# Mixer network on one Trainium2 core: the last batch's row lists summed on TensorE from one-hots, and the second expert stage's first loads reordered

## The reference, cut to what matters

```python
logits = x @ gate_weight.T                 # 2048 tokens, 128 experts
logits = where(old_to_new == -1, -inf, logits)
top_v, top_i = top_k(softmax(logits), 8);  top_v /= sum(top_v)
flat_e = old_to_new[top_i].reshape(-1)     # 48 kept experts
oh  = flat_e[:, None] == arange(48)
pos = sum(cumsum(oh, axis=0) * oh, axis=-1) - 1     # place within the expert
valid = pos < 192
xb[flat_e, pos] = x[tok]
g, u = split(einsum('ech,eoh->eco', xb, gate_up_proj))
y = einsum('eci,ehi->ech', silu(g) * u, down_proj)
final[tok] += y[flat_e, pos] * top_v * valid
x = layernorm(x + final)
```

## Time and profile before

| | |
|---|---|
| median of 3 runs | 2162.5 us (2161.75 to 2166.09) |
| time of the profiled execution | 2158.87 us |
| its span | 2157.1 us |
| PE busy | 1739.3 us (81%) |
| DVE busy | 1523.6 us (71%) |
| ACT busy | 956.8 us (44%) |
| POOL busy | 1086.7 us (50%) |

### The profile page before, as it was taken

The page is one execution under the profiler, slowest core; times in us unless marked ns, Lnnn a source line. Parts: engine busy times, 40 slices in busy tenths (PEclk is TensorE's granted clock), DMA queues, the critical chain, the costliest instruction groups (busy, mean ns, idle before and its releaser), DMA issues. The chain is left out here.

```text
span 2157.1 us, 34592 instructions
## 1 busy us (share of the span) xinstructions
PE 1739.3 (81%) x9155; PEld 1383.7 (64%) x9156; DVE 1523.6 (71%) x2883; ACT 956.8 (44%) x1867; POOL 1086.7 (50%) x817
## 2 busy tenths in 40 slices
PE   4898989347999999999998888788832079999990
PEld 3566565236888888888886555555421078888880
DVE  4477777765777888887884323788879757777774
ACT  4355452312444444444443324444423157777773
POOL 1000624564667667667676000044538657777763
PEclk9899989657999999999999898888865589999995
DMA  8011111035888888888896613131010369999967
GB/s 322 28 40 59 31 48 40 1 122 152 206 208 212 205 227 211 223 228 212 218 231 153 198 21 59 59 59 59 1 59 23 126 194 256 258 250 256 257 149 254
DMA packets 138553, 318.80 MB, mean 148 GB/s; under 512 B 30713, under 2 KB 31321, under 8 KB 136825
## 3 DMA queue, kind: packets, MB, share of 16 engines
q1 hardware_dynamic: 71448, 201.74, 27.1%
q0 software_dynamic: 64752, 112.04, 26.8%
q10 hardware_dynamic: 2288, 4.29, 0.5%
HBM read 238.68 MB, written 97.62 MB: 156 GB/s over the span
## 5 line engine op out<-in xcount | busy, mean ns | idle before, releaser
L98 POOL DMA_INDIRECT tab_rows<-pair,slot x256 | 313.7, 1226 | 452.6 <-DVEq L752 296.6
L90 PE MATMUL gu<-wgu_h,xgT_h 128*128 x648 | 233.5, 360 | 7.3 <-DVE xgT_l L1428 3.7
L1253 POOL DMA_INDIRECT xg<-x_rows,ids x167 | 191.5, 1147 | 62.5 <-issue 48.5
L90 PE MATMUL gu<-wgu_l,xgT_h 128*128 x648 | 219.6, 339 | 0.0
L90 PE MATMUL gu<-wgu_h,xgT_l 128*128 x648 | 218.3, 337 | 0.0
L1308 ACT ACTIVATE ysb<-yp,wts 128x512 f32<-128x512 f32 x160 | 110.1, 688 | 144.7 <-PE yp L1535 144.7
L90 PE MATMUL guk<-xgT_hk,wgu_hk 128*128 128x192 f32 x576 | 161.7, 281 | 0.0
L90 PE MATMUL guk<-xgT_lk,wgu_hk 128*128 128x192 f32 x576 | 158.8, 276 | 0.0
L90 PE MATMUL guk<-xgT_hk,wgu_lk 128*128 128x192 f32 x576 | 158.8, 276 | 0.0
L1298 ACT ACTIVATE sg<-gu 128x192 f32<-128x192 f32 x162 | 53.6, 331 | 235.1 <-PE gu L90 235.1
L1428 DVE TENSOR_TENSOR xgT_l<-tpx,xgT_h 128x512 fp32r<-128x512 f32 x163 | 112.2, 688 | 55.6 <-ACT xgT_h L1294 53.4
(11 more groups left out here) (503 smaller groups left out, 5043.3 us busy)
## 6 DMA issues: line engine op xcount, KB each, us to landing
wgu_sb<-in_wgu SPq DMA_DIRECT2D x64, 768.0 KB
wgu_sbk<-in_wgu SPq DMA_DIRECT2D x48, 768.0 KB, 4.4
wd_sb<-in_wd SPq DMA_DIRECT2D x64, 256.0 KB
wd_sbk<-in_wd SPq DMA_DIRECT2D x48, 256.0 KB, 5.3
ct<-in_ctxT SPq DMA_DIRECT2D x8, 1024.0 KB, 5.0
wd_sb<-in_wd SPq DMA_DIRECT2D x64, 128.0 KB
wd_sbk<-in_wd SPq DMA_DIRECT2D x48, 128.0 KB, 5.8
odd_rows<-zero SPq DMA_DIRECT2D x1, 4352.0 KB, 15.5
```

Source lines behind the costliest of these rows:

```text
L90: i = nc.tensor.matmul(out, left(k), right(k), start=(start and k == 0 and m == 0), stop=(k == ops - 1 and m == 2))
L98: nc.gpsimd.indirect_dma_start(out=tab, out_offset=bass.IndirectOffsetOnAxis(ap=s["slot"][:, n:n + 1].bitcast(U32), axis=0), in_=s["pair"] ...
L1253: nc.gpsimd.indirect_dma_start(out=xg[:, t % G, :], out_offset=None, in_=x, in_offset=bass.IndirectOffsetOnAxis(ap=ids[:, t:t + 1].bitcast ...
```

## The change

1. The last batch's four tiles are routed together, as the other batches are. Its pairs are not scattered. SP loads the table as it is after three batches (in a tile of `x3`), ahead of the last batch's stores; DVE makes its token numbers float before it routes.
2. `hot` of the last batch lies in `parts`, a bf16 tile of 32 choices x 5 values x 48 experts, experts innermost: the one-hot itself, the one-hot times the token number, and the one-hot times the weight in three bf16 pieces. For each choice, `spots` is the one-hot of its position among 192 places. 64 products on TensorE (32 choices, places in two groups of 128 and 64) sum `spots` transposed times `parts` over tokens and choices in one PSUM tile, which holds for each place and expert the row number and weight. `lists_taken` adds them to the transposed table of the three batches and writes `ids` and `wts`, which now are made before `kept_experts` starts.
3. `kept_experts` starts with the gathers. The rows are cleared in four parts, one per expert pair of halves, and gathers wait for their part alone. ACT and DVE take expert 0's rows before its weights. SP requests the third expert's weights when the rows of the first two experts have landed.

```diff
@@ kept_experts, SP @@
                 if e >= 2:
                     sp.wait_ge(s_wt[e % 2], e // 2 * 48)
+                if e == 2:
+                    for m in range(2):
+                        sp.wait_ge(s_g[m], 32)
@@ kept_experts, POOL @@
-            scatter(nc, tab, s, E1 * REG1 - 1, s_lot, BT - 1)
...
+                elif t % 2 == 0:
+                    pool.wait_ge(s_clear, t // 2 + 1)
...
-            pool.wait_ge(s_tab, 3)
@@ kept_experts, ACT @@
             for n in range(2):
+                copy_xT(0, n)
                 gate_up_upper(0, n, False)
                 down_upper(0, n, False)
-            act.wait_ge(s_lot, SCAT)
-            nc.scalar.dma_start(lot[:, :, :].rearrange("t n o -> t (n o)"),
-                                tab.rearrange("(r n) o -> r (n o)", n=P)[0:T1, :]).then_inc(s_rows, 16)
-            copy_xT(0, 0)
-            copy_xT(0, 1)
@@ kept_experts, DVE @@
-            nc.vector.memset(xg[:, :, :], 0.0).then_inc(s_tab, 1)
+            for n in range(NF):
+                nc.vector.memset(xg[:, 2 * n:2 * n + 2, :], 0.0).then_inc(s_clear, 1)
...
             for n in range(2):
+                split_xT(0, n)
                 gate_up_lower(0, n)
                 down_lower(0, n)
@@ mixer_two, SP @@
+                        sp.wait_ge(s_scat, (B - 1) * (16 * BT * TOPK))
...
+                        sp.dma_start(lot.rearrange("t n o -> t (n o)"),
+                                     d["tab1"].rearrange("(r n) o -> r (n o)", n=P)[0:T1, :]).then_inc(s_lot, 16)
@@ mixer_two, POOL @@
+            nc.gpsimd.iota(places[:, :], [[1, CAP]], base=0, channel_multiplier=0,
...
-            for j in range(BT - 1):
-                pool.wait_ge(s_idx, B + j + 1)
-                settle(pool, passed)
-                scatter(nc, d["tab1"], drain, E1 * REG1 - 1, s["lot"][1], j, j + 1)
@@ mixer_two, DVE, drained @@
-                for j in range(BT):
-                    route_j(j)
-                    slots_j(j)
...
+                dve.wait_ge(s_lot, 16)
+                c.done(nc.vector.tensor_copy(lotf, lot[:, :, 0]))
+                routed()
+                parts_made()
+                spots_made()
+                lists_taken()
@@ mixer_two, DVE, parts_made @@
+                    c.done(nc.vector.tensor_tensor(parts[:, :, 1, :].rearrange("p (j k) e -> p e j k", k=TOPK),
+                                                   own.rearrange("p e (j k) -> p e j k", k=TOPK),
+                                                   tok16[:, :].unsqueeze(1).unsqueeze(3).to_broadcast([P, E1, BT, TOPK]), ALU.mult))
...
+                    c.done(nc.vector.tensor_tensor(parts[:, :, 2:5, :].rearrange("p n v e -> p v e n"), own.unsqueeze(1).to_broadcast([P, 3, E1, NP]),
+                                                   w16[:, :, :].unsqueeze(2).to_broadcast([P, 3, E1, NP]), ALU.mult))
@@ mixer_two, DVE, spots_made @@
+                    for n in range(NP):
+                        nc.vector.tensor_scalar(spots[:, n, :], places[:, :], pos8[:, n:n + 1], None, ALU.is_equal).then_inc(s_spot, 1)
@@ mixer_two, PE, drained @@
+                for n in range(NP):
+                    pe.wait_ge(s_spot, n + 1)
+                    for m, (lo, w) in enumerate(((0, P), (P, IR))):
+                        i = nc.tensor.matmul(tb[0:w, m, 0:5 * E1].rearrange("p (v e) -> p v e", e=E1), spots[:, n, lo:lo + w],
+                                             parts[:, n, :, :], start=(n == 0), stop=(n == NP - 1))
+                i.then_inc(s_list, 1)
```

More of the change, by code:

```diff
@@ L1576, in kept_experts @@
         ysb = sb("ysbk", [P, G, D])
-        lot = sb("lotk", [T1, P, 2], I32)
-        lotf = sb("lotfk", [T1, P])
-        ids = sb("idsk", [P, T1], I32)
-        wts = sb("wtsk", [P, T1])
+        ids, wts = s["ids"], s["wts"]
         tpx = ps("tpxk", [P, 2, 512])
@@ L2361, in norm3, with route_rows @@
                 assert c.n == N2, c.n
-            def route_rows(c, js, logits, at):
+            def route_rows(c, js, logits, hot):
                 rows = slice(js[0] * TOPK, (js[-1] + 1) * TOPK)
@@ L2448, in route @@
                 dve.wait_ge(s_lg, b + (ROUTED + 1))
-                yield from route_rows(c, range(BT), lgp, 0)
+                yield from route_rows(c, range(BT), lgp, hot)
                 assert c.n == KRT, c.n
@@ L2473, in drained @@
                 stat, mv, rstd, shift = stats[2]
+                own = parts[:, :, 0, :].rearrange("p n e -> p e n")
                 c.done(nc.vector.tensor_scalar(tokf[:, :], tokf[:, :], float(S), None, ALU.add))
+                c.done(nc.vector.tensor_scalar(back[:, :], s["tcol"][:, 0:1], -1.0, -float(2 * P), ALU.mult, ALU.add))
                 dve.wait_ge(s_x4, B * BT)
@@ L2518, in drained @@
                 scaled(3)
-                for j in range(BT):
-                    route_j(j)
-                    slots_j(j)
-                with nc.allow_low_precision("small counts"):
-                    for j in range(BT):
-                        c.done(nc.vector.tensor_tensor(s["macc1"][:, :], s["macc1"][:, :], mask[:, j, :], ALU.add))
-                        c.wait()
+                dve.wait_ge(s_lot, 16)
[4 more added lines that the diff above has]
+                lists_taken()
             norm1(0, True)
@@ L2870, in program @@
         mixer_one(nc, d, s)
+        sb, _, _ = alloc(nc, ctx)
+        s.update(ids=sb("idsk", [P, T1], I32), wts=sb("wtsk", [P, T1]))
         with ExitStack() as held:
```

146 lines of the change are left out of this document (91 added, 55 removed).

## The result

| | kernel before | changed kernel |
|---|---|---|
| median (lowest to highest), us | 2162.12 (2155.89 to 2166.09), 4 runs | 2201.85 (2196.46 to 2206.18), 4 runs |
| ratio, 95% interval | 1 | 1.0185 [1.0151, 1.0219] |
| profiled execution: its time, its span | 2158.87, 2157.1 | 2203.19, 2201.3 |
| mark (lower half of expert 3's weights on DVE) | 1751.46 | 1789.16 |
| mark to the end of the span | 405.6 | 412.1 |

The change makes the kernel 39.7 us slower. The forecast was no difference, and the time lies far outside its range. Of the 44.2 us between the two spans 37.7 have gathered by the mark.

What follows compares the result with a forecast made beforehand. Bound: the path through POOL's last 32 scatters and the table's load to the second expert stage's even pace. First gather 12.6 us earlier, 6.3 given back, 5.7 lost to strided reads: 0.6 faster, 2161.9 us; own range 2158.5 to 2165.5, overall 2154.5 to 2168.

Steps and rivals of the forecast that it cites:

- load of the table, start of the routing: After DVE's last scatter lands, SP loads the 96 KB table in 2.2 us with its issue; routing starts at 1677.65.
- routing up to `mask`'s end, with the strides: DVE routes four tiles in the third batch's 14.56 us, +0.8 for strided `hot`, +0.96 for `mask`'s strided reads.
- the parts, with the strides: On DVE: small operations 1.6, token product 1.76, three-piece product 4.9, sum 8.2 us; strided reads add 0.96 and 2.87.
- gather to the first gate product: Gathers share DMA with the first two experts' weights: +2.4 us; weights split behind the rows: +1.3.
- gate product to the mark: From first gate product to expert 3's lower half on DVE: 12.4 us instead of 9.8, so +2.6.
- The stride: DVE's reads of one-hots 480 bytes apart cost 0.62 ns a number more, 5.7 us, leaving 0.6 of 6.3 us gained.
- a rival with chance 0.12: Strided writes of `hot` and both parts products pay too: 4.8 us more, in total 4.2 slower, 2166.7; chance 0.12.
- Comparisons and product: 32 DVE comparisons, 6.0 us, beside 64 PE products, 21 at 0.20 and 43 at 0.10 us: 8.8 us.
- the rise after 4.3 us: PE kept busy rises to 2.4 GHz after 4.3 us, as in `kept_experts`; then 43 products take 0.10 us each.
- the bound of 13.1: Upper bound in us for comparisons and 64 products, where PE's clock stays low, against 8.8 forecast.
- The rival on the clock: PE's clock stays low through the 64 products because PE idled before: 3.7 us slower, 2166.2; chance 0.07.
- The held request: Rival: it doesn't free the gathers; rows land with experts 0 and 1's weights, 8 for 5.5 us: 1.9 slower, 2164.4; chance 0.06.

Runs made afterwards that it cites:

- e15_two: Change with pieces written in expert runs tile by tile, late table wait and four experts' weights requested early; two bf16 weight pieces instead of three: 64 products 18.41 us, ratio 1.0000.
- e8_tiles_warm: Change with pieces written in expert runs tile by tile and late table wait, plus 22 added products of 512 columns before the 64: these take 19.63 us, ratio 1.0013.
- e3_nohold: The change without the wait of the third expert's weights for the first rows: ratio 1.0187.
- e18_change_even: The change with four experts' weights requested at the mixer's end, the fifth's held for the first rows, each expert's rows split before its weights: ratio 1.0151.

## Why the prediction was wrong, point by point

Forecast mark 1750.9 (1751.46 less 0.6), measured 1789.16: 38.3 us to explain, from the rows above.

| step of the prediction | forecast | measured | difference |
|---|---|---|---|
| load of the table, start of the routing | 1677.65 | 1677.87 | +0.2 |
| routing up to `mask`'s end, with the strides | 16.3 | 21.9 | +5.6 |
| the parts, with the strides | 12.0 | 29.3 | +17.3 |
| `where` and its sum, with the stride | 5.5 | 5.85 | +0.3 |
| comparisons and 64 products | 8.8 | 21.3 | +12.5 |
| the lists | 2.4 | 2.15 | -0.2 |
| lists to the first gather | 3.2 | 2.6 | -0.6 |
| gather to the first gate product | 12.6 | 15.3 | +2.7 |
| gate product to the mark | 12.4 | 12.85 | +0.5 |

- **The stride** failed, by 23 us. The prediction saw that writes 480 bytes apart were new, made them a rival with chance 0.12, and priced a written number like a read one, 0.62 ns on top, from the row of `pos`. Measured, a lone bf16 number takes 4.6 ns in all: `hot` 7.07 for 1.76, the token product 7.05 for 2.7, three pieces 20.98 for 7.8 (10.7 if the rival held). The turning point it gave, 0.08 ns a written number, was passed nearly forty times over: 22.8 us on 7680 written numbers, 3.0 ns each on top of the forecast. `pos` writes 32 numbers; no row of the kernel before wrote apart, so the upper bound was no bound of a write, and the sign of being wrong that it named (the three-piece product under 6 us) looked only the other way. The strided reads came as taken: `mask` 3.00 for 2.7, `where` 3.06 for 2.7.
- **Comparisons and product** failed, by 12.5 us. The comparisons were right (5.83 us for 6.0). The product's 0.20 us were only its columns; each carries 0.128 more (e15_two). The price was drawn from products of 48 columns 0.04 us apart that have none of this. And the clock did not rise (granted 0.50): "the rise after 4.3 us" was read from other products, and the bound of 13.1, called where the clock stays low, left out the 0.128. 64 x 0.328 = 21.0. The rival on the clock held, but its reason, that PE idled before, is at best half of it (e8_tiles_warm), and it was priced at 4.3 us, a third of what the stage lost.
- **The held request** neither helped nor harmed (e3_nohold). The second gather came 8.25 us late, the rival's 8, behind the weights of experts 0 and 1, requested from 1758.98 to 1761.55. With four experts' weights requested before the lists, and the fifth held, the rows of e18_change_even reach PE 5.1 us sooner and the mark comes 7.1 us sooner behind the gather.
- **The load of the table, the routing's bf16 chain, lists and seam** stood within 0.6 us each.
- **What lies behind the mark** was taken as fixed. The even step held up to 1860 us and then now and then took 7.8 to 8.1; the profile has 6.5 us more behind the mark, the medians 2.0 (39.7 less 37.7). Why is not shown.

From the cast to the lists the change needs 80.7 us of DVE and PE one behind the other (1677.73 to 1758.4); the kernel before had its lists at 1731.88.

## What to carry to other kernels

Before a layout is turned so that a product may read neighbours, price the write that fills it: bf16 numbers written alone cost 4.6 ns each at any distance tried from 16 to 480 bytes, runs of four nothing extra, and the loop order of the operation that writes (experts innermost here) gives both sides neighbours for one 1.4 us copy. Cost a train of products by the distance between starts of products like them, with weights that change each time, and at the clock that such products were seen to hold. And when a chain is shortened, see what it covered: beside its last scatters and the table's load the kernel before fetched six experts' weights, and only when four were again asked for ahead of the lists, and the fifth held behind the rows, did the rows come in time.

## What the runs showed of the hardware that I had not expected

- A bf16 number written alone, 16 to 480 bytes from the next: 4.4 to 4.7 ns; an f32 number 128 bytes or more from the next 2.0; a pair of bf16 in one word 2.2; runs of four bf16 as fast as dense (0.56 us for 768 numbers).
- PE's reads of its moving columns 64 bytes apart: 0.511 us for 240 columns instead of 0.328, at the lower level.
- PE busy without a gap for 21 us with 64 products of 240 columns: granted clock 0.50 throughout; started at 1.00, it fell while PE was busy (1.00 to 1744, 0.57 from there to 1748, 0.50 behind, e8_tiles_warm). With the experts' products it rose and stayed (1.00 from 1790 to 1860 us in the change).
- A gather of POOL beside DVE's subtractions: 3.49 us instead of 0.98.
- Two copies of ACT on four of the five chips: 2.2 to 5.2 us idle ahead of each, mostly with no releaser in the trace; why is not known.
